# A decoder layer on one core: expert tiles written out, both kinds of turns at a step's head, first gathers inside the early tiles, late tiles summed one step later

## What is computed

```python
x = x + attention(layernorm(x)); x = x + cross_attention(layernorm(x), ctx)
def ffn(x):                                   # x = layernorm(x) of 4096 tokens
    logits = affine_layernorm(x) @ gate_w.T   # 8 experts
    probs = softmax(logits); top 2 of 8, renormalized -> w[:, e]
    out = swiglu(x, sWg, sWu, sWd)            # shared expert, every token
    for e in range(8):
        out = out + w[:, e:e+1] * swiglu(x, Wg[e], Wu[e], Wd[e])
swiglu(x, wg, wu, wd) = silu(x @ wg) * (x @ wu) @ wd     # 256 -> 512 -> 256
```

## Time and profile before

| what | us |
|---|---|
| timed runs | 1702.4, 1705.21, 1707.19 |
| median | 1705.21 |
| the profiled execution's own time | 1713.24 |
| its span, first to last instruction | 1711.5 |
| PE busy | 1663.2 (97% of the span) |
| DVE busy | 1381.4 (81%) |
| ACT busy | 1097.7 (64%) |
| GpSimd (POOL) busy | 395.4 (23%) |

### The profile page before, as it was taken

How to read it: one execution, slowest core, us unless ns; L and a number is a source line. 1 busy time by engine, 2 the same in 40 slices (tenths; PEclk the granted TensorE clock), 3 DMA queues, 4 the chain that set the end, 5 groups by cost and what they waited for, 6 DMA issues and landing times. The chain is left out here.

```text
span 1711.5 us, 35350 instructions
## 1 busy us (share of the span) xinstructions
PE 1663.2 (97%) x11830; PEld 1092.0 (64%) x11831; DVE 1381.4 (81%) x2605; ACT 1097.7 (64%) x2272; POOL 395.4 (23%) x464
## 2 busy tenths in 40 slices
PE   7899999999999999999989999997999999999998
PEld 3443333333333333358678999996898888888887
DVE  6788999999999999926678889994887666666664
ACT  5336888888888888872567777874335545454552
POOL 2000000000000000023042222222562555554540
PEclk9858999999999999999999999998999999999999
DMA  6601112221111111012311222113725333333335
GB/s 218 197 11 21 31 31 39 38 36 33 33 31 31 31 30 30 3 43 75 119 44 45 101 67 84 49 50 118 244 76 167 53 55 50 55 49 55 50 58 169
DMA packets 85147, 116.41 MB, mean 68 GB/s; under 512 B 19051, under 2 KB 64415, under 8 KB 84415
## 3 DMA queue, kind: packets, MB, share of 16 engines
q1 hardware_dynamic: 67248, 90.95, 19.2%
q0 software_dynamic: 13728, 18.88, 6.7%
q10 hardware_dynamic: 4047, 4.91, 0.9%
HBM read 71.25 MB, written 46.60 MB: 69 GB/s over the span
## 5 line engine op out<-in xcount | busy, mean ns | idle before, releaser
L506 DVE TENSOR_REDUCE half_max<-psA 128x1 f32<-128x512 f32 x1024 | 630.9, 684 | 20.1 <-PE psA L559 18.1
L538 ACT ACTIVATE PT<-psB 128x1024 f32<-128x1024 f32 x512 | 520.8, 1026 | 154.0 <-PE psB L569 153.5
L559 PE MATMUL psA<-KS,QS 48*128 48x512 f32 x1024 | 404.9, 479 | 8.2 <-PEq L104 2.5
L569 PE MATMUL psB<-QS,KS 50*128 50x512 f32 x1024 | 384.8, 465 | 0.1
L588 PE MATMUL psO<-PT,VG 128*32 128x256 f32 x4096 | 327.6, 399 | 0.1
L559 PEld LDWEIGHTS psA<-KS,QS 48*128 48x128 f32 x1024 | 166.6, 195 | 238.9 <-DVE half_max L506 178.0
L588 PEld LDWEIGHTS psO<-PT,VG 128*32 128x32 f32 x4096 | 85.2, 109 | 180.4 <-issue 109.3
L1390 ACT ACTIVATE x_probs<-x_scores,x_neg_max 128x77 f32<-128x77 f32 x512 | 176.3, 358 | 6.8 <-DVE x_neg_max L1293 6.6
L569 PEld LDWEIGHTS psB<-QS,KS 50*128 50x128 f32 x1024 | 154.0, 189 | 10.7 <-ACT PT L538 9.5
L1872 PE MATMUL m_psY<-swd_high,m_hT 128*128 128x256 f32 x760 | 157.6, 290 | 0.3 <-DVE m_hT L2026 0.2
L475 POOL CAST max_parts<-neg_max 128x16 fp32r<-128x16 f32 x32 | 6.3, 196 | 632.1 <-DVE neg_max L516 632.1
(11 more groups left out here) (235 smaller groups left out, 2702.5 us busy)
## 6 DMA issues: line engine op xcount, KB each, us to landing
QS<-q_parts SPq DMA_DIRECT2D x96, 128.0 KB
q_parts<-part SPq DMA_DIRECT2D x16, 512.0 KB, 4.4
mx_kept<-cx_mx SPq DMA_DIRECT2D x8, 616.0 KB, 4.9
cx_mx<-mx_kept SPq DMA_DIRECT2D x4, 1232.0 KB, 7.4
KS<-k_parts SPq DMA_DIRECT2D x32, 128.0 KB
xf_rows<-XF SPq DMA_DIRECT2D x32, 128.0 KB, 1.7
acc<-X SPq DMA_DIRECT2D x32, 128.0 KB, 1.8
xf_turned<-n_xfT SPq DMA_DIRECT2D x32, 128.0 KB, 1.8
```

Of the source, the lines that this page charges most:

```text
L506: dve.tensor_reduce(half_max[:, h * (TB // 2) + t % (TB // 2), n:n + 1], psA[:, bank_of(slot, 2 * v + r), :], axis=AX.X, op=ALU.max).then_ ...
L538: act.activation(PT[:, k % 4, 2 * a:2 * a + 2, :].rearrange("p h n -> p (h n)"), psB[:, u % 2, :, :].rearrange("p a n -> p (a n)"), ACT.Ex ...
L559: pe.matmul(psA[:, bank_of(slot, m), :], QS[top:top + KQ, slot, h // 2, t * P:(t + 1) * P], KS[top:top + KQ, slot, n * HALF:(n + 1) * HALF ...
L569: mm = pe.matmul(psB[:, u % 2, r, :], KS[top:top + KM, slot, c * P:(c + 1) * P], QS[top:top + KM, slot, a, half * HALF:(half + 1) * HALF], ...
```

## The change

Four edits in the mixture stage. First, steps 28 to 93 are written out like the others, so that no loop and no tile number in a register is left. Second, the two turns of tile s's tokens move from behind the gate and up products to the step's head, right behind the hidden turns. Third, the gathers run two tiles ahead, not one, and the first two are issued while early tiles 22 and 23 run. Fourth, DVE adds the partial sum of a late tile in step i+3 instead of i+2.

```diff
--- before.py
+++ after.py
@@ -1430,6 +1430,7 @@
 EARLY_TILES = 24
 LATE = NT - EARLY_TILES
 END = EARLY_TILES + NTM
+LATE_SUM = 3
 NALL = END + LATE
 COPIES = 6
 COUNT_AT = 3
@@ -1642,10 +1643,7 @@
             for s in range(EARLY_TILES + 4):
                 step(lambda lag, s=s: (s - lag, (s - lag) % 2) if s >= lag else None)
                 beside(s)
-            with eng.Fori(EARLY_TILES // 2 + 2, END // 2) as j:
-                for e in range(2):
-                    step(lambda lag, j=j, e=e: (j * 2 + (e - lag), (e - lag) % 2))
-            for s in range(END // 2 * 2, NALL + 2):
+            for s in range(EARLY_TILES + 4, NALL + LATE_SUM):
                 step(lambda lag, s=s: (s - lag, (s - lag) % 2) if s - lag < NALL else None)
 
         def turned_tile(i, e):
@@ -1799,12 +1797,14 @@
                     weight_half_low(s - POOL_FROM)
                 if 0 <= s - HOT_AT < NHOT:
                     hot_values(s - HOT_AT)
+                if s == EARLY_TILES - 2:
+                    pool.wait_ge(slots_done, 6)
+                if s >= EARLY_TILES - 2:
+                    gather(s + 2)
             pool.wait_ge(lows_pool, POOL_LOWS + POOL_HALVES)
-            pool.wait_ge(slots_done, 6)
-            gather(EARLY_TILES)
             for i in range(EARLY_TILES, END + 2):
-                if i + 1 < END:
-                    gather(i + 1)
+                if i + 2 < END:
+                    gather(i + 2)
                 if i == EARLY_TILES + 2:
                     for e in range(2):
                         pool.wait_ge(stored[e], 16 * (EARLY_TILES // 2))
@@ -1830,6 +1830,13 @@
                     for k in range(KF):
                         mm = pe.transpose(psH[:, 0, k * P:(k + 1) * P], SG[:, e, k * P:(k + 1) * P], ident[:, :])
                     mm.then_inc(ht_done, 1)
+                if (t := tile(0)) and not shared(t[0]):
+                    i, e = t
+                    pe.wait_ge(gathered[e], at(i - e, 8, 16 - 8 * EARLY_TILES))
+                    wait_low(pe, i - 1)
+                    for k in range(KD):
+                        mm = pe.transpose(psT[:, 0, k * P:(k + 1) * P], xt[:, e, k * P:(k + 1) * P], ident[:, :])
+                    mm.then_inc(t_done, 1)
                 if t := tile(1):
                     i, e = t
                     if isinstance(i, int) and i == EARLY_TILES:
@@ -1845,13 +1852,6 @@
                                 mm = pe.matmul(bank[:, e, :], xT[a][:, e, k, :], w, start=(k == 0 and (a, b) == PRODUCTS[0]),
                                                stop=(k == KD - 1 and (a, b) == PRODUCTS[-1]))
                         mm.then_inc(done, 1)
-                if (t := tile(0)) and not shared(t[0]):
-                    i, e = t
-                    pe.wait_ge(gathered[e], at(i - e, 8, 16 - 8 * EARLY_TILES))
-                    wait_low(pe, i - 1)
-                    for k in range(KD):
-                        mm = pe.transpose(psT[:, 0, k * P:(k + 1) * P], xt[:, e, k * P:(k + 1) * P], ident[:, :])
-                    mm.then_inc(t_done, 1)
                 if t := tile(2):
                     i, e = t
                     if not shared(i):
@@ -2041,15 +2041,18 @@
                 if beside:
                     second_piece(now[0])
                     dve.sem_inc(pieces_done, 1)
-                if t := tile(2):
-                    i, e = t
-                    dve.wait_ge(y_done, at(i, 1, 1))
-                    if shared(i):
+                for lag, late in ((2, False), (LATE_SUM, True)):
+                    if (t := tile(lag)) and shared(t[0]) and (t[0] >= END) == late:
+                        i, e = t
                         n = number(i)
-                        bank = 0 if i < EARLY_TILES else e
+                        bank = e if late else 0
+                        dve.wait_ge(y_done, at(i, 1, 1))
                         dve.wait_ge(acc_in[n % 2], 16 * (n // 2 + 1))
                         dve.tensor_tensor(yt[:, n % 3, :], psY[:, bank, 0:D], yt[:, n % 3, :], ALU.add).then_inc(y_in, 1)
-                    else:
+                if t := tile(2):
+                    i, e = t
+                    if not shared(i):
+                        dve.wait_ge(y_done, at(i, 1, 1))
                         if peeled(i, EARLY_TILES + 2):
 
                             dve.wait_ge(stored[(i - 3) % 2], 16 * ((i - 3) // 2 + 1))
```

More of the change, by code:

```diff
@@ L2043, in step @@
                     dve.sem_inc(pieces_done, 1)
+                for lag, late in ((2, False), (LATE_SUM, True)):
+                    if (t := tile(lag)) and shared(t[0]) and (t[0] >= END) == late:
+                        i, e = t
+                        n = number(i)
+                        bank = e if late else 0
+                        dve.wait_ge(y_done, at(i, 1, 1))
+                        dve.wait_ge(acc_in[n % 2], 16 * (n // 2 + 1))
+                        dve.tensor_tensor(yt[:, n % 3, :], psY[:, bank, 0:D], yt[:, n % 3, :], ALU.add).then_inc(y_in, 1)
                 if t := tile(2):
                     i, e = t
-                    dve.wait_ge(y_done, at(i, 1, 1))
-                    if shared(i):
-                        n = number(i)
-                        bank = 0 if i < EARLY_TILES else e
-                        dve.wait_ge(acc_in[n % 2], 16 * (n // 2 + 1))
-                        dve.tensor_tensor(yt[:, n % 3, :], psY[:, bank, 0:D], yt[:, n % 3, :], ALU.add).then_inc(y_in, 1)
-                    else:
+                    if not shared(i):
+                        dve.wait_ge(y_done, at(i, 1, 1))
                         if peeled(i, EARLY_TILES + 2):
```

## The result

The changed kernel takes 1694.87 us (median of 9 runs, 1693.13 to 1697.51), the kernel before, timed beside it on the same chip, 1704.14 (9 runs, 1699.01 to 1717.26). The ratio is 0.9945, 95% interval 0.992 to 0.997: faster by 0.55%. The forecast was 1700.0 in a range from 1695.5, so the direction was right and the time lies 0.6 us under the range.

What follows compares the result with a forecast made beforehand. The prediction took a ring through ACT, DVE and the split down weights' single buffer to bound expert steps; -5.5 written out and +0.3 at the tail gave -5.2 us, scaled to a 1700.0 us median, range 1695.5 to 1706.

Steps and rivals of the forecast that it cites:

- Written out: Expert tiles: without the loop each of 70 steps takes 4.93 for 5.01 us, saving 5.5 us (4.1 to 6.2).
- The branch: The loop's branch behind the odd step's Y: the trace shows no cost there, so nothing was added for it.
- Turns at the head: Token turns on PE, 0.19 us a step, are moved, not removed; PE waits at Y anyway: zero gain.
- The doubt about the new wait at the head: Step's head: the wait for the preceding tile's low token part keeps 0.22 us of room; if late, G, U, Y queue.
- Gathers: GpSimd's gathers go out a step earlier, turns need them 3.23 us earlier; room grows by 1.7 us, effect zero.
- Late sums: Late tiles: DVE's shift frees nothing; later stores and copies on SP cost 0.3 us at the end (0 to 2.7).
- The sum: Whole span against the profiled execution: -5.5 + 0.3 = -5.2 us, 1706.3 for 1711.5.
- Rival 1: Expert steps: PE is the bound after all, steps take 4.83 us, time 1692.9 us; chance 0.10.
- the ring: Expert step: Y, ACT's `swd_high`, DVE's `swd_low`, DVE's low hidden part, Y, through one weight buffer; 4.93 us a step.
- Rival 2: Loop's even steps: their delay stays in part or is smaller unprofiled; 1 to 3 us gained, about 1703; chance 0.13.
- Rival 3: Written-out steps: PE's instructions arrive late, about 13 fetches at 0.8 us each, 1710 us; chance 0.04.
- Rival 4: Late tiles: the shifted SP queue delays loads, ACT waits 2 us in each of the last four, 1708; chance 0.03.

Runs made afterwards that it cites:

- experiment 4: The change with the two token turns back behind the gate and up products: 1695.1 us, ratio 0.9957.
- experiment 1: The kernel before with only its loop written out: 1695.68 us, ratio 0.9958.
- experiment 3: The change with the late tiles' partial sums added at their old step, i+2: 1701.37 us, ratio 0.9997.
- experiment 5: The change with the gathers back to one tile ahead, the first two behind the early tiles: 1717.79 us, ratio 1.0086.
- experiment 9: The kernel before with its loop written out and Y's four products with the low hidden part last: 1696.7 us, ratio 0.9953.

## Why the prediction was right, and where it failed

**Written out: right.** Steps of 4.93 were forecast, 345.1 for 70; the loop written out alone has 345.02, the change 345.71; the turns at the head make this difference (experiment 4: 345.05). One step, at tile 52, is 5.26, 0.33 too long: DVE's `swd_low` there waited 1.16 for ACT, not 0.81. Experiments 1 and 4 have the same long step, and the loop has one too (5.29, at tile 28).

**The branch: as the rows said.** The price in the Trainium skill ("Advanced Engine Details and Errata", Control Flow Timing), some 108 ns a compare-and-branch, would by an estimate from that page have made the gain 5.5 + 3.6 = 9.1. The first experiment removes the branches and the stalls together and gains 350.63 - 345.02 = 5.6.

**Turns at the head: zero, right.** Experiment 4 shows it, with 0.66 us against them. The doubt about the new wait at the head was unfounded with early gathers.

**Gathers: the sum right, its reasons wrong.** The room was said to grow by 1.7 and the gathers to cost nothing. They had two effects that the step did not see: from the add at 1577 on, adds run behind one another (a loss of 5.3, shown in experiment 3), and without them the turns at the head would lose 18.6 (experiment 5). They also took along 0.49 of tile 95's wait for its down weights: marks 94 to 95 are 4.71 to 4.72 in the kernels with earlier gathers and 5.18 to 6.32 in those without. The traces point to the last add. The weights' loads go out at the same place in both. Where the last add starts 5.9 to 6.3 after the mark of tile 94, behind them, the second of the two lands after 4.7 to 4.9; where it starts 2.4 to 2.5 after it, while they are under way, after 5.4 to 6.3. No run moves this add alone.

**Late sums: right for the tail, wrong for the rest.** The end moved by 0.24 where 0.3 was forecast. But "DVE's shift frees nothing" took late steps as they were before the gathers moved; with them moved, the late sum saves 5.3, 1.6 of it low clock behind the stall. Both errors are equal and opposite: it is luck that the sum did not show them.

**The sum: right, in part by luck.** -5.2 was forecast for the span; the marks give -5.3. The expert steps give -4.9 for -5.5, and the -0.6 at tiles 95 and 96 was not foreseen.

**The time: the failed step** is "The median of the runs shown, 1705.21, is 0.5% under that execution; the same difference gives 1700.0", together with the lower end of the range. It took three runs as the level of the kernel before and left out the clock near the start, which no term of the sum holds. They span 4.8 us; the nine runs of before have their median at 1704.14, the later 32 at 1702.45 and those of the 32 at a mean clock of 0.983 at 1701.08. Six of the change's nine runs are at this clock, and none is below 0.982. So of the 5.1 us by which 1700.0 was too high, 4.1 is the level (1705.21 for 1701.08), 0.1 the sum, and 0.9 stays open. That none of the nine had a longer low-clock stretch is luck as far as the runs show: 20 of the 32 runs of before have 0.982 or more, and 8 of the 12 of experiment 4, which differs from the change only in the place of the turns. The lower end of the range allowed for the spread of three runs, not for where they stood in the spread of all.

**The rivals.** Rival 1 is wrong for the change (steps of 4.94, ended by DVE) and right for the kernels in which the ring is cut. Rival 2 did not occur: experiment 1 gains in timed runs what the profile shows. Rival 3: instructions were fetched, 20 packets on q8 between 1300 and 1650 where 13 were counted, and at most one step was longer. An instruction packet of q14 stands at that step (1444); that the one made the other was not tried. Rival 4: late tiles stayed at 4.64.

## What to carry to other kernels

Find the ring that sets a step, follow it with durations, and cut it; an edit that only moves work on an engine that waits is worth nothing until then, and may be worth much after. Edits that are worth nothing together can be large with opposite signs: take each back by itself before calling it idle. Where a few runs of one kernel spread over as much as the change is worth, read the clock of each and forecast the difference between stages, not the median.

## What the runs showed of the hardware

PE's low-clock stretch near the start lasted some 75 us in one execution and some 40 in another, with the same code, and a whole run's time goes with it: 1699.93 to 1702.19 at a mean clock of 0.983, 1714.82 at 0.974. What sets its length is not known from these runs. One stall late in the kernel cost more than itself: after 3.51 us without work PE was granted the lower level (0.50 from 1668 to 1670 in experiment 3), and the step behind the stall took 6.28 for 4.64.

A chain of indirect adds, each waiting for the one before, runs at about the pace of the steps: after one delay of 1.0 us at 1577 the 15 adds behind it kept some 1.3 us of lateness, which neither grew nor went. In experiment 9, where two steps of 5.1 and 5.9 came by, the adds caught up. While the chain runs, an add takes some 4.2 us from issue to landing, where it takes 3.8 to 3.9 otherwise, and its issue 1.9 to 2.0 instead of 1.59.

A wait on a register instruction ahead of a matmul costs 0.13 us against the same wait on the matmul; 33 of them would make 33 x 0.13 = 4.3 of the 5.6 us that the written-out loop saves. The rest, and what the loop's branch has in it, was not taken apart.
